# Cross-attention of a decoder layer on one core: pieces of G one place earlier, two transposed contexts, x1 transposed into the FFN operand's place

## The reference

```python
x = layernorm(x + self_attention(x))                # one head of 256
Q = x @ Wq.T + bq;  K = ctx @ Wk.T + bk              # 1024 wide
attn = softmax(Q @ K.T / 32)                        # per batch (112, 375)
x = layernorm(x + attn @ ctx)                       # the context itself is attended
h = silu(x @ Wg) * (x @ Wu)                         # 4-bit weights, scales per group of 128, inner width 2752
x = layernorm(x + h @ Wd)
```

## Time and profile before

| | |
|---|---|
| runs shown | 1948.92, 1944.59, 1948.36 us; median 1948.36 |
| profiled execution | 1946.6 us, span 1944.9 us, granted TensorE clock 0.989 |
| busy in the span | TensorE 1824.9 us (94%), VectorE 887.3 (46%), ScalarE 430.2 (22%), GpSimd 350.6 (18%) |
| cross-attention | first logits 393.7 us, batch 14's logits 682.8 us, first FFN product 722.8 us |

### The profile page before, as it was taken

One profiled execution on the slowest core, in us unless ns is written; L12 is line 12 of the kernel. 1 busy time (PEld: TensorE's weight loads), 2 busy tenths in 40 slices (PEclk: granted clock), 3 DMA queues, 4 the chain that ended last, 5 costly groups with the idle time before them and its releaser, 6 DMA issues.

```text
span 1944.9 us, 26655 instructions
## 1 busy us (share of the span) xinstructions
PE 1824.9 (94%) x10214; PEld 1023.1 (53%) x10214; DVE 887.3 (46%) x1342; ACT 430.2 (22%) x660; POOL 350.6 (18%) x261
## 2 busy tenths in 40 slices
PE   4898899888888969999999999999999999999998
PEld 2666644577767734444445444444545444444443
DVE  5688641668878864443443444344343311111111
ACT  3222110444444422222222222222222200000000
POOL 0222377212222211121111112111111000000000
PEclk9999999999999979999999999999999999999999
DMA  9242761479999953112111211212121321221220
GB/s 309 76 143 77 190 192 43 96 167 236 235 236 251 219 100 65 44 34 59 35 44 38 56 44 34 59 35 44 37 54 40 116 102 53 102 102 69 85 102 22
DMA packets 300527, 196.67 MB, mean 101 GB/s; under 512 B 260024, under 2 KB 274552, under 8 KB 298300
## 3 DMA queue, kind: packets, MB, share of 16 engines
q1 hardware_dynamic: 294236, 192.85, 39.2%
q10 hardware_dynamic: 6240, 3.15, 0.6%
HBM read 105.30 MB, written 50.80 MB: 80 GB/s over the span
## 4 chain that ended last, share of the span: by engine, by line
PE 51%; issue 32%; DVE 8%; POOL 4%; DMA 3%; ACT 1%; SPq 1%; POOLq 0%; DVEq 0%; ACTq 0%
PE psum L1276 49%; POOL arena L1016 2%; DMA arena<-in_x 2%; POOL small L942 1%; DVE arena L715 1%; PE psum L1485 1%; POOL arena L951 1%; DMA arena<-in_L_xattn_Wq 1%; DMA x_parts_scratch<-arena 1%; PE psum L1503 1%; PE psum L1269 1%; DVE arena L830 1%; DVE arena L495 1%; DVE small L684 0%; DVE small L410 0%
## 5 line engine op out<-in xcount | busy, mean ns | idle before, releaser
L1276 PE MATMUL psum<-arena 128*128 128x448 f16 (+9 forms) x9432 | 1753.0, 347 | 60.2 <-POOL arena L1016 15.7
L1276 PEld LDWEIGHTS psum<-arena 128*128 128x128 f16 (+5 forms) x9432 | 973.8, 106 | 820.5 <-issue 104.6
L1040 POOL TENSOR_TENSOR arena<-arena 128x1024 f16<-128x1024 f32 (+1 forms) x65 | 138.3, 2128 | 692.7 <-ACT arena L1218 692.7
L883 DVE SCALAR_TENSOR_TENSOR arena<-psum,small,arena 128x448 f32<-128x448 f32 x84 | 57.4, 684 | 409.0 <-PE psum L1276 409.0
L924 DVE SCALAR_TENSOR_TENSOR arena<-psum,small,arena 128x512 f32<-128x512 f32 x28 | 21.0, 750 | 333.1 <-PE psum L1276 320.9
L942 POOL TENSOR_TENSOR small<-small 112x1 f32<-112x1 f32 (+1 forms) x46 | 37.0, 804 | 588.5 <-DVE small L384 588.4
L1218 ACT ACTIVATE arena<-arena 128x1024 f16<-128x1024 f32 (+1 forms) x65 | 68.7, 1057 | 277.8 <-DVE arena L869 277.8
L1231 ACT ACTIVATE arena<-arena 128x448 f16<-128x448 f32 (+1 forms) x88 | 50.7, 576 | 291.9 <-DVE arena L883 291.9
L1016 POOL TENSOR_TENSOR arena<-arena 128x224 f16<-128x224 f32 x64 | 62.0, 969 | 144.4 <-ACT arena L1137 144.4
L889 DVE TENSOR_TENSOR arena<-arena 128x448 f16<-128x448 f32 (+1 forms) x88 | 55.0, 625 | 57.5 <-ACT arena L1231 57.5
L867 DVE TENSOR_TENSOR arena<-arena,psum 128x1024 f32<-128x1024 uint32 x65 | 79.4, 1221 | 2.6
(11 more groups left out here) (179 smaller groups left out, 750.0 us busy)
## 6 DMA issues: line engine op xcount, KB each, us to landing
h_scratch<-arena SPq DMA_DIRECT2D x88, 224.0 KB, 2.9
arena<-h_scratch SPq DMA_DIRECT2D x13, 1408.0 KB, 6.1
arena<-in_ctx SPq DMA_DIRECT2D x32, 512.0 KB, 4.5
arena<-in_x SPq DMA_DIRECT2D x32, 448.0 KB, 5.7
x_scratch<-arena SPq DMA_DIRECT2D x32, 448.0 KB, 3.5
arena<-in_L_ffn_down_qweight SPq DMA_DIRECT2D x21, 512.0 KB
x_parts_scratch<-arena SPq DMA_DIRECT2D x16, 448.0 KB, 5.5
arena<-in_ctx SPq DMA_DIRECT2D x16, 448.0 KB
```

Of the source, the lines that this page charges most:

```text
L883: dve.scalar_tensor_tensor(h_f[0:n, :], up[0:n, :], sc_u[0:n, :], g_act[0:n, :], ALU.mult, ALU.mult).then_inc(s_hf, 1)
L1040: pool.tensor_tensor(dst[1], src, dst[0], ALU.subtract).then_inc(s_wl, 1)
L1276: mm = pe.matmul(out, a, r, start=(k == 0), stop=(k == len(pairs) - 1))
```

## The change

- TensorE: the pieces of G are shifted by one. Nine stand ahead of the first logits; in batch n come pieces 4n+9 and 4n+10 behind the logits, 4n+11 ahead of the attended sum, and 4n+12 behind the maximum. The loop over groups is written out for all 16 batches. ScalarE's `g_out` follows the same order, the last one behind the three high parts of the context.
- Two transposed contexts: `cxt` has two places, the second where `xtp` was. Context n+1 is transposed in batch n without waiting for the logits of n.
- x1 is transposed into `x2t`'s columns of its own batch (`x1t = x2t`), all 16 batches once: pairs 0 to 4 ahead of the loop, the first not before M and its row sums on GpSimd are done, pairs 5, 6 and 7 at the end of batches 0, 1 and 2.
- VectorE: the low parts of context n+1 are written at the beginning of batch n, between the steps of the normalisation and the softmax, no longer those of n+2 at its end. `row_term` writes its unused output into PSUM (banks 0 and 1) and waits for no store; `add_attended` waits for it instead.
- x2's split: ScalarE writes the permuted and scaled rows in float32 (`x2f`), then rounds them to float16; GpSimd subtracts. `x2p` has one slot.
- The spread maxima are put into bank 4 instead of bank 2; the transposes of the probabilities wait for the read.
- SyncE: context n+2 is loaded in batch n chunk by chunk, with the transposes of context n+1 between.

The buffers and VectorE's part (`normalise` now has `context_lo(n + 1, (b + 1) % GB, 0)` ahead of its last step, where it had `context_max`):

```diff
-        cxt = carve(at_ctxt, [2, KC, CTXP], F16)
+        cxt = [carve(at, [2, KC, CTXP], F16) for at in (at_ctxt, at_xt)]
+        x1t = x2t
...
             def row_term(n, b):
                 dve.wait_ge(s_xr3[b % 2], slot_fills(n, b))
-                dve.wait_ge(s_yout[b % 2], 16 * NB // 2 + slot_fills(n, b))
-                if not known(n, 2):
-                    dve.wait_ge(s_lo, n - 1)
-                dve.tensor_tensor_reduce(yo[0:S, b % 2, :], xr3[0:S, b % 2, :], u_b[0:S, :], 1.0, 0.0,
+                dve.tensor_tensor_reduce(psum[0:S, 0:D], xr3[0:S, b % 2, :], u_b[0:S, :], 1.0, 0.0,
...
             def cross_attention(g, more):
                 for b, n, has in batches(g, more):
+                    if not known(n, 1):
+                        normalise(n - 1, (b + 3) % GB, n + 1 if has(1) else None)
+                        if has(1):
+                            context_lo(n + 1, (b + 1) % GB, 1)
                     softmax_in(n, b)
-                    if not known(n, 1):
-                        normalise(n - 1, (b + 1) % 2, n + 2 if has(2) else None)
-                    else:
+                    if has(1) and not known(n, 1):
+                        context_lo(n + 1, (b + 1) % GB, 2)
+                    if has(2):
                         context_max(n + 2, 0)
+                    if has(1):
+                        row_term(n + 1, (b + 1) % GB)
+                    probs_lo(n)
                     if has(2):
                         context_max(n + 2, 1)
-                    probs_lo(n)
-                    if has(2):
                         context_max(n + 2, 2)
-                    if not known(n, 1):
-                        x2_lo(n - 1, b + 1)
                     add_attended(n, b)
                     if has(2):
                         context_largest(n + 2)
                         context_factor(n + 2, (b + 2) % GB)
-                    if has(2):
-                        context_lo(n + 2, (b + 2) % GB, 0)
-                    if has(1):
-                        row_term(n + 1, (b + 1) % GB)
-                    if has(2):
-                        context_lo(n + 2, (b + 2) % GB, 1)
-                    if has(2):
-                        context_lo(n + 2, (b + 2) % GB, 2)
```

GpSimd, called ahead of each batch's last `g_lo`, and TensorE:

```diff
+            def x2_lo(n):
+                pool.wait_ge(s_hi, n + 1)
+                pool.tensor_tensor(x2p[0:S, 1, :], x2f[0:S, :], x2p[0:S, 0, :], ALU.subtract).then_inc(s_lo, 1)
...
+            def cross_attention(n):
+                b = n % GB
+                logits(n, b)
+                if n + 2 < NB:
+                    g_chunk(KC + 4 * n + 1)
+                    g_chunk(KC + 4 * n + 2)
+                probs_t(n)
+                if n + 2 < NB:
+                    g_chunk(KC + 4 * n + 3)
+                attended(n, b)
+                if n + 2 < NB:
+                    largest_of_context(n + 2)
+                if n + 3 < NB:
+                    g_chunk(KC + 4 * n + 4)
```

SyncE, ahead of the loop and in it (`load_x1t(q)` issues the two transposes of pair q, `load_cxt(c, s)` that of chunk c into place s):

```diff
             next_ctx(1)
-            load_cxt(0, 0)
-            next_ctx(2)
+            sp.wait_ge(s_m, KC)
+            sp.wait_ge(s_uc, 4 * KC)
+            sp.wait_ge(s_pu, 2 * KC)
+            sp.wait_ge(s_selo, 16)
+            load_x1t(0)
+            sp.wait_ge(s_ub, 1)
+            for c in range(CC):
+                load_cxt(c, 0)
+            for q in range(1, 5):
+                load_x1t(q)
...
+            def cross_attention(g, more):
+                for b, n, has in batches(g, more):
+                    for c in range(CC):
+                        if has(1):
+                            sp.wait_ge(s_cl, CC * (n + 1) + c + 1)
+                        if has(2):
+                            load_ctx(n + 2, c)
+                        if c == 0:
+                            if not known(n, 1):
+                                store_x2(n - 1, (b + 1) % 2)
+                                sp.wait_ge(s_l, n)
+                            else:
+                                sp.wait_ge(s_v, 2 * NG)
+                            sp.sem_inc(s_due, 1)
+                        if has(1):
+                            load_cxt(c, (b + 1) % 2)
+                    if not has(1):
+                        sp.wait_ge(s_l, NB)
+                        load_chunk(0, 0, P)
+                        load_chunk(1, 1, P)
+                    if not known(n, 1):
+                        load_x2t(n - 1)
+                    if has(2):
+                        sp.wait_ge(s_y3, 2 * (n + 1))
+                        load_residual(n + 2, (b + 2) % GB)
+                    if known(n, 3):
+                        load_x1t(5 + n)
```

More of the change, by code:

```diff
@@ L270, in decoder_layer @@
         s_x1h = sem("x1_hi_ready"); s_x1l = sem("x1_lo_ready")
-        s_x1o = [sem(f"x1_parts_out{i}") for i in range(2)]; s_x1t = [sem(f"x1T_half{q}_in") for q in range(2)]
+        s_x1o = [sem(f"x1_parts_out{i}") for i in range(2)]; s_x1t = [sem(f"x1T_pair{q}_in") for q in range(NB // 2)]
         s_xr3 = [sem(f"x1_residual_in{i}") for i in range(2)]
@@ L293, in decoder_layer @@
         s_cx = [sem(f"ctx_chunk{c}_in") for c in range(CC)]
-        s_ct = sem("ctxT_in"); s_due = sem("ctxT_due")
+        s_ct = [sem(f"ctxT_slot{i}_in") for i in range(2)]; s_due = sem("ctxT_due")
         s_g = sem("g_in_psum"); s_ge = sem("g_copied"); s_re = sem("row_term_ready")
@@ L301, in decoder_layer @@
         s_y3 = sem("sum3_ready"); s_hi = sem("x2_hi_ready"); s_lo = sem("x2_lo_ready")
-        s_x2t = [sem(f"x2T_slot{i}_in") for i in range(2)]
+        s_x2t = sem("x2T_in"); s_x2f = sem("x2_f32_permuted")
         s_qw = [sem(f"qw_in{i}") for i in range(2)]; s_tc = [sem(f"tabc_in{i}") for i in range(2)]
@@ L739, in add_attended @@
                 dve.wait_ge(s_rc3, 2 * n + 2)
+                dve.wait_ge(s_yout[b % 2], 16 * NB // 2 + slot_fills(n, b))
+                if not known(n, 2):
+                    dve.wait_ge(s_lo, n - 1)
                 for h in range(2):
@@ L749, in normalise @@
                 if beside is not None:
[L750 removed]
+                    context_lo(beside, (b + 2) % GB, 0)
                 norm_apply(y, NB + n, s_n)
@@ L1022, in cross_attention @@
                     if has(2):
-                        for k in range(4):
+                        for k in range(3):
                             g_lo(KC + 4 * n + k, 4 * (b % 2) + k, 1 - b // 2)
+                    if not known(n, 1):
+                        x2_lo(n - 1)
+                    if has(2):
+                        g_lo(KC + 4 * n + 3, 4 * (b % 2) + 3, 1 - b // 2)
             pool.wait_ge(s_mm, 2)
@@ L1212, in high_part @@
                 if kind == 2:
-                    for i in range(2):
-                        act.wait_ge(s_x2t[i], 16 * (NB // 2 + 1))
+                    act.wait_ge(s_x2t, 16 * NB)
                 src = wbuf[kind]
@@ L1419, in attended @@
                                                 for r in range(CC) for w, a in PASSES]).then_inc(s_at, 1)
-            def cross_attention(g, more):
-                for b, n, has in batches(g, more):
-                    logits(n, b)
-                    if has(2) and b % 2 == 0:
-                        pe.wait_ge(s_x1t[1 - b // 2], 32 * (g + 1 + b // 2))
-                    if has(2):
-                        pe.wait_ge(s_ge, KC + 4 * n - 1)
-                        if not known(n, 1):
-                            pe.wait_ge(s_cf, 4 * (n + 1) + 1)
-                        g_chunk(4 * (b % 2), 1 - b // 2)
-                    if has(2):
-                        pe.wait_ge(s_ge, KC + 4 * n)
-                        g_chunk(4 * (b % 2) + 1, 1 - b // 2)
-                    probs_t(n)
-                    if has(2):
-                        pe.wait_ge(s_ge, KC + 4 * n + 1)
-                        g_chunk(4 * (b % 2) + 2, 1 - b // 2)
-                    attended(n, b)
-                    if has(2):
-                        pe.wait_ge(s_ge, KC + 4 * n + 3)
-                        largest_of_context(n + 2)
-                    if has(2):
-                        g_chunk(4 * (b % 2) + 3, 1 - b // 2)
+            def cross_attention(n):
[12 more added lines that the diff above has]
+                    g_chunk(KC + 4 * n + 4)
             pe.wait_ge(s_me, KC + 2)
@@ L1457, in _ @@
                         mm.then_inc(s_g, 1)
-            for y in range(2, KC):
-                pe.wait_ge(s_ge, y - 1)
-                g_chunk(y, 0)
+            for k in range(2, KC + 1):
+                g_chunk(k)
             pe.wait_ge(s_ube, 1)
-            cross_attention(0, True)
-            with pe.Fori(1, NG - 1) as g:
-                cross_attention(g, True)
-            cross_attention(NG - 1, False)
+            for n in range(NB):
+                cross_attention(n)
             def free_banks(q):
@@ L1513, in chunk @@
                     if t == 3:
-                        for k in range(2):
-                            pe.wait_ge(s_x2t[k], 16 * (NB // 2 + 1))
+                        pe.wait_ge(s_x2t, 16 * NB)
```

(15 more changed lines are left out.)

100 lines of the change are left out of this document (42 added, 58 removed).

## The result

Four runs of the changed kernel took 1976.76 to 1981.66 us, median **1978.02 us**, against 1946.47 us for the kernel before in the same comparison: ratio 1.0162, 95% interval 1.0145 to 1.0179. It is slower by 31.55 us. The direction was forecast, the size was not: 1955 us was predicted, and 1978 us lies above the range of 1922 to 1972 us. The profiled execution took 1977.2 us, its span is 1975.5 us, the granted TensorE clock 0.969.

The account below looks back on a forecast made before the run. Neither TensorE nor VectorE filled the 20.64 us period; waits did. With 13 rounds of 21.1 us, +4 and -1, batch 14's logits came at 689.5 instead of 682.76 us, +6.7 us: 1955 us, range 1922 to 1972.

Parts of the forecast that it names:

- Steps 1 and 2: TensorE in the cross-attention: G's pieces one place earlier and two transposed contexts remove waits of 13.8 and 10.5 us.
- Step 3: x2's low part leaves VectorE for ScalarE and GpSimd: VectorE saves 2.00 us per batch, cost taken as nothing.
- Step 4: Row term written to PSUM no longer waits for x2's store: 12.8 us of VectorE's idle time go.
- Step 5: New order of context loads and transposes: a closed ring decides the period, 21.1 us against 20.64 now.
- the ring: Per batch: low part, SyncE's transposes and chunk loads, VectorE to next low part; 21.1 us, bounds 18.9 to 22.6.
- Step 6: x1's transposes moved on SyncE: at most 1 us at the start, +4 us for the last six.
- rival A: Transposes issue quickly with other transfers between them: ring 18.9 us, 1926 us; chance 0.24.
- Step 7: Unrolled TensorE code, semaphores, banks: nothing; the tail keeps the same chain as before.
- +4 and -1: Terms of the sum: +4 us for x1's transposes, -1 us since logits start earlier within the round.
- C: First transpose held as long as the longest row, up to 4.79 us: ring 22.6 us, 1974 us; chance 0.14.
- B: Engines bound: context maximum comes late but VectorE catches up, period 18 us, 1915 us; chance 0.12.

## Why the prediction was wrong, step by step

- **Steps 1 and 2 (G's pieces, two contexts)** were right as far as the waits go: both kinds are gone in the change, and none appeared for G even with turns of 19.7 us (those for a transposed context came back there, 20.9 us). What they are worth shows only without the long ring: 13 to 16 us with the loads first (1932.83 and 1929.74 us against 1946.1), in which steps 3 and 4 are included. How this divides between steps 1 and 2 was not tried.
- **Step 3 (x2's low part)** was costed at nothing. In the change itself that can't be seen. With the loads first it is worth 6.4 us, by two kernels whose intervals overlap a little. ScalarE's two passes took 2.09 and 1.06 us, GpSimd's subtraction 2.13 us; GpSimd did not become late.
- **Step 4 (row term)** right: 1.30 us on average in PSUM (1.49 before), and the wait it removes is worth nothing by itself, as its own run shows; the time that counted was TensorE's.
- **Step 5 (the ring)**: the mechanism is right, and **its size is what failed**. The terms, forecast and measured (means of the 13 turns, the start from the later ten):

| term | forecast | measured |
|---|---|---|
| low part's end to first transpose | 1.5 | 1.9 |
| first transpose | 3.55 | 4.84 |
| issue of chunk 1 | 0.7 | 0.7 |
| second transpose | 3.03 | 3.61 |
| gaps | 0.4 | 0.2 |
| chunk 2 to VectorE | 4.3 | 4.7 |
| VectorE | 7.6 | 7.4 |
| sum | 21.1 | 23.3 |

  From the last maximum of one turn to that of the next it is 23.47 us over twelve turns (430.05 to 711.71); the 0.15 us more are x1's transposes, see step 6. By L1417 it is 23.65, since batch 1 isn't yet in the ring. The sum is 2.2 us too short, and 1.3 of them are the first transpose. "I take 3.55, the nearest case" was the mistake: that row stood behind context loads alone, while the transpose of the turn has a chunk *and* the store of x2 moving, and the run with the store moved shows 3.42 us for a chunk alone. It was also one row of several: in the kernel before, eight first transposes stood directly behind context loads in the loop and held the queue 3.13 to 4.79 us, 3.71 on average. 0.4 us more is GpSimd's power, which I had put beside the statistics: VectorE waits 0.45 us for it ahead of L397. The second transpose was taken from x2's, which follow another transfer (the store, 448 KB, and not a chunk of 512 KB), and cost 0.6 us more. The bounds of the transposes were not far off (4.84 against 4.79, 3.61 against 3.27), but the other terms were given no upper ends, so that the ring's upper bound was 22.6 us.
- **The Trainium skill's rate** (DMA: Bandwidth & Descriptors, Latency and other measured facts; 261 GB/s for a DMA transpose with a non-contiguous middle dimension) leads to an estimated 1921 us, further down than rival A's 1926. As a measure of the hold the trace after disagrees with it more than the one before: 36 transposes of L1701 held the queue 3.24 to 5.54 us, median 3.75, so 512 KB at 140 GB/s.
- **Step 6 (x1's transposes)**: the start was right (first G product 368.08 us, probabilities of batch 0 0.7 us later than before). The +4 us were 1.7 us: in two turns x1's transposes hold the queue past the end of the first low part, and the first transpose starts 2.95 and 2.54 us behind it instead of 1.9. SyncE's queue in the second of them (the low part ended at 460.91 us):

```profile
457.30 4.94 SPq L1615 DMA_TRANSPOSE arena<-x_parts_scratch  x2
462.28 0.58 SPq L1675 DMA_DIRECT2D arena<-in_ctx  x1
462.91 0.43 SPq L1720 DMA_DIRECT2D x_scratch<-arena  x1
463.45 5.54 SPq L1701 DMA_TRANSPOSE arena<-arena  x1
```

  The ring had turned out longer than forecast, which leaves the queue more time to get through. With shorter turns they cost more, as the turn of 26.5 us shows.
- **Step 7** right: the tail is unchanged, as both 31.1 us above show.
- **The sum**: 12 turns by 2.55 us more (+30.6, x1's 1.7 among them), the thirteenth only 18.3 instead of 21.1 us because no piece of G stands between its maximum and batch 14's logits (-2.8), no separate +4 and -1 (-3.0): 24.8 us. Forecast 689.5 + 24.8 gives 714.3 for batch 14's logits; measured 713.84.
- **The rivals**: C had the right mechanism and nearly the right size (ring 22.6, 1974 us) and got 0.14. Its 22.6 us needs both transposes at their upper bounds, though its words speak of the first alone, which gives 22.3. A and B, with 0.36, needed quick transposes, and none in the change that stood behind a chunk and the store took under 4.52 us; that the first could be *slower* than 3.55 stood in the spread of the earlier trace rows. The range ended at 1972 us, just below C's own time, with no room for the ends of the other terms.

## What to carry to other kernels

Where a queue that is issued strictly in order feeds a single buffer, write down the closed ring (buffer free, issue, landing, use, free) before moving a load: two transposes put ahead of one load cost 45 us here against the same transfers in the other order. Put the loads that free the ring first, and take for an issue that holds its queue the price measured behind the same neighbours in the queue, or its upper bound where no row has them, not one row or the median. A wait removed on an engine that isn't last, as the 12.8 us of the row term, is worth nothing until what hides it is gone.

## What the runs showed of the hardware that was not expected

- How long a DMA transpose of 512 KB holds its queue depends on what moves ahead of it: 4.84 us on average behind a chunk and a store (960 KB), 3.42 us behind one chunk (512 KB), 1.69 to 3.00 us behind another transpose and 28 KB. The amount alone doesn't set it: with the loads first, the first transpose has three chunks (1.5 MB) ahead of it and held the queue 4.0 us on average over 13 turns.
- Alternating transposes and loads is dearer than grouping them. Three transposes with a load between each held SyncE 12.0 us on average over 13 turns of the change (5.53 + 3.89 + 4.14 = 13.6 in the turn shown, the longest); with the loads first, 9.0 us. SyncE's queue in one turn there, where the three take about as long as in the earlier trace rows:

```profile
518.59 0.35 SPq L1720 DMA_DIRECT2D x_scratch<-arena  x1
519.78 0.36 SPq L1675 DMA_DIRECT2D arena<-in_ctx  x1
523.06 0.34 SPq L1678 DMA_DIRECT2D arena<-in_ctx  x1
523.59 0.29 SPq L1679 DMA_DIRECT2D arena<-in_ctx  x1
523.93 8.80 SPq L1701 DMA_TRANSPOSE arena<-arena  x3
```

- The granted clock fell where TensorE waited: 0.90 in 500 to 550 us of the change (38.57 of 50 us busy), 0.83 with three transposes ahead (36.99 of 50), 1.00 with none ahead (47.30 of 50). The group of 96 products that took 10.88 us in the row of 409.54 us, without a wait ahead of it, took 13.07 us in the row of 432.10 us, behind a wait of 4.58. These 2.2 us fill only time in which the ring is being waited for anyway, and the FFN behind it has the full clock again (1.00 from 760 to 1000 us).
